# One transpose for queries and keys, one transfer for the row maxima, and a new order of a decoder layer on one core

## What is computed

```
x = layernorm(x + favor_attention(x))         # 16 heads of 16; exp features of 64 per head, kv and its
                                              # sum over each sequence of 128 rows, num/den, then Wo
x = layernorm(x + cross_attention(ctx, x))    # 16 heads of 16, softmax over the 128 rows of ctx
x = layernorm(x + ffn(x))                     # ternary weights 256->1024->256, activations quantized to
                                              # 127 levels by the row's largest magnitude, tanh-based silu
```

## Time and profile before

| | |
|---|---|
| time before, median of 3 runs | 506.53 us (505.39 to 511.43) |
| the profiled execution | 505.92 us, its span 504.2 us |
| mean granted TensorE clock | 0.967 |
| busy: PE / DVE / ACT / POOL | 438.9 / 450.6 / 428.8 / 365.5 us |
| DMA: all packets | 192659, 64.27 MB, mean 127 GB/s |

### The profile page before, as it was taken

How to read it: one execution, slowest core, us unless ns; L and a number is a source line. 1 busy time by engine, 2 the same in 40 slices (tenths; PEclk the granted TensorE clock), 3 DMA queues, 4 the chain that set the end, 5 groups by cost and what they waited for, 6 DMA issues and landing times.

```text
span 504.2 us, 18524 instructions
## 1 busy us (share of the span) xinstructions
PE 438.9 (87%) x6566; PEld 304.7 (60%) x6566; DVE 450.6 (89%) x1355; ACT 428.8 (85%) x908; POOL 365.5 (72%) x789
## 2 busy tenths in 40 slices
PE   4568888998999998999999999999999999876641
PEld 2235666666776766776767676777676766543310
DVE  4667686999999999899999999999999999999771
ACT  2247789999999998999999999999999999867532
POOL 1447767778788888788888888888888876763422
PEclk9979899999999999999999999999999999999875
DMA  7665566787768787566666666666666687542212
GB/s 186 230 125 101 133 116 109 107 154 124 127 130 134 157 140 133 133 146 146 146 146 141 140 139 135 144 140 142 136 145 136 137 139 127 85 75 62 55 33 63
DMA packets 192659, 64.27 MB, mean 127 GB/s; under 512 B 172384, under 2 KB 192352, under 8 KB 192608
## 3 DMA queue, kind: packets, MB, share of 16 engines
q1 hardware_dynamic: 190080, 60.46, 60.4%
q10 hardware_dynamic: 2528, 3.15, 1.7%
HBM read 17.31 MB, written 4.19 MB: 43 GB/s over the span
## 4 chain that ended last, share of the span: by engine, by line
PE 58%; ACT 13%; DMA 11%; DVE 7%; issue 5%; SPq 3%; POOL 3%; ACTq 0%; POOLq 0%; DVEq 0%
PE bank L1131 10%; PE bank L1335 9%; DMA tT<-pkT 4%; PE bank L1306 4%; PE bank L1225 4%; PE bank L1362 4%; PE bank L1183 3%; DMA ffn_ld<-in_L_ffn_w_down_dram 3%; PE bank L1204 2%; PE bank L1145 2%; PE bank L1240 2%; PE bank L1322 2%; PE bank L1150 2%; PE bank L1211 2%; PE bank L1294 2%
## 5 line engine op out<-in xcount | busy, mean ns | idle before, releaser
L1131 PE MATMUL bank<-wq_hi,xT 128*128 128x512 f16 (+1 forms) x256 | 72.5, 338 | 3.7 <-DVE vv L816 2.3
L434 POOL TENSOR_TENSOR ve<-mv,lneps 128x1 f32<-128x1 f32 x96 | 19.4, 202 | 63.4 <-DVE mv L866 48.0
L438 POOL TENSOR_TENSOR rs<-ve,mhalf 128x1 f32<-128x1 f32 x96 | 55.0, 573 | 0.0
L946 DVE SCALAR_TENSOR_TENSOR g<-th,bank 128x512 f32<-128x512 f32 x64 | 43.4, 678 | 4.7 <-ACT th L653 4.3
L558 ACT ACTIVATE x<-y,nmr,rs 128x256 f32<-128x256 f32 x64 | 39.8, 622 | 7.9 <-DVE y L1007 4.4
L630 ACT ACTIVATE pT<-bank 128x512 f32<-128x512 f32 x64 | 37.8, 591 | 9.7 <-PE bank L1296 8.1
L897 DVE TENSOR_REDUCE negm<-bank 128x4 f16<-128x512 f32 x64 | 43.4, 678 | 1.6 <-PE bank L1260 1.2
L898 DVE TENSOR_REDUCE negm<-bank 128x4 f16<-128x512 f32 x64 | 43.5, 680 | 0.0
L577 ACT ACTIVATE phk<-bank 128x512 f32<-128x512 f32 x64 | 39.4, 617 | 4.5 <-PE bank L1150 4.5
L1131 PE MATMUL bank<-wq_lo,xT 128*128 128x256 f16 (+1 forms) x128 | 43.2, 337 | 0.0
L425 POOL TENSOR_TENSOR pkA<-qk,pkA 128x512 f16<-128x512 f32 x32 | 37.6, 1175 | 7.0 <-ACT pkA L520 6.6
(11 more groups left out here) (184 smaller groups left out, 1580.0 us busy)
## 6 DMA issues: line engine op xcount, KB each, us to landing
xs<-in_x_dram SPq DMA_DIRECT2D x32, 128.0 KB, 2.3
cs<-in_ctx_dram SPq DMA_DIRECT2D x32, 128.0 KB, 2.3
xr<-in_x_dram SPq DMA_DIRECT2D x32, 128.0 KB, 2.3
out_dram<-ot SPq DMA_DIRECT2D x32, 128.0 KB, 1.8
ffn_ld<-in_L_ffn_w_gate_dram ACTq DMA_DIRECT2D x1, 1024.0 KB, 9.0
ffn_ld<-in_L_ffn_w_up_dram ACTq DMA_DIRECT2D x1, 1024.0 KB, 11.5
ffn_ld<-in_L_ffn_w_down_dram ACTq DMA_DIRECT2D x1, 1024.0 KB, 13.8
pkAT<-pkA SPq DMA_TRANSPOSE x64, 3.2
```

The source lines that it names most:

```text
L438: g.tensor_tensor(rs[n - 1][:, :], ve[n - 1][:, :], mhalf[:, :], ALU.pow).then_inc(done[f"pw{n}"], 1)
L946: v.scalar_tensor_tensor(g1[:, n, :], th[:, n, :], 1.0, gate, ALU.add, ALU.mult).then_inc(done[f"gl{n}"], 1)
L1131: last = T.matmul(o, xT[:, 2 * part + c, :], w[:, c, cols], start=(n == 0), stop=(n == 5))
```

## The change

- `qT` and `kT` become one DMA transpose of 128 x 2048, `qT`, at the place of the old `qT`; it waits for `lo`, `nlo` and for `phq1` of the tile before. `kT` and its semaphores are gone.
- The row maxima go into 16 packed columns (negm of 128 x 16, not 128 x 128), their transpose has 16 rows (nmT), and `row` is one DMA from these 16 rows into partitions 32 and 96.
- The banks are given out anew, and with them the waits that protect them; some waits and increments that others imply are dropped.
- Every engine's order is new: `LAGS` is 14, `FIRST` is 18. Much of the shift of lags is only where an iteration is said to begin. What moves against its neighbours: on PE `phk0` and `phk1` go behind `s0`, `kvp` goes ahead, `st0` behind `nump`, `vm` to the end; on ACT `p0` goes ahead of `x2_`, `th0` ahead of `x1_`, `sq` behind `x1T_`, `kvm_` before it, `hm1` ahead of `hm0`, `ot_` between `ephq0` and `ephq1`; on POOL `lo` goes ahead of `xqf`, `xb_` two iterations earlier; on SP the order is qT, tT_, load_x, store, cT_, load_r, load_c, hqT_, row. The ffn preparation is spread otherwise over the first iterations.

The core of the diff (the lists of the engines shown for SP and ACT):

```diff
-LAGS = 13
-FIRST = 16
+LAGS = 14
+FIRST = 18
...
-        negm = sb("negm", [P, 2, 64], F16)
+        negm = sb("negm", [P, 2, PAIRS], F16)
...
             def qT(t, par):
-                wait_ahead(sp, t, par, ("phq0", -1))
-                transpose(pkAT[:, 0:PAIRS, :], pkA[:, 0:PAIRS, :, :].rearrange("p c r d -> p (c r d)"), "qT", par)
-
-            def kT(t, par):
-                wait_ahead(sp, t, par, ("lo", 0), ("nlo", 0), ("phk0", -1))
-                transpose(pkAT[:, PAIRS:H, :], pkA[:, PAIRS:H, :, :].rearrange("p c r d -> p (c r d)"), "kT", par)
+                wait_ahead(sp, t, par, ("lo", 0), ("nlo", 0), ("phq1", -1))
+                transpose(pkAT[:, :, :], pkA[:, :, :, :].rearrange("p c r d -> p (c r d)"), "qT", par)
...
             def row(t, par):
                 wait(sp, "mT", t)
-                for p in (32, 96):
-                    sp.dma_start(tT[p:p + 1, par, :, :], nmT[p:p + PAIRS, :]).then_inc(moved["row"][par], 16)
+                sp.dma_start(tT[32:P:64, par, :, :], nmT[:, :]).then_inc(moved["row"][par], 16)
...
-                go(load_c, i, par, 4)
-                go(load_r, i, par, 4)
+                go(qT, i, par, 4)
+                go(tT_, i, par, 7)
                 go(load_x, i, par, 0)
-                go(kT, i, par, 3)
+                go(store, i, par, 14)
+                go(cT_, i, par, 6)
+                go(load_r, i, par, 2)
+                go(load_c, i, par, 5)
                 go(hqT_, i, par, 10)
-                go(store, i, par, 13)
                 go(row, i, par, 7)
-                go(qT, i, par, 3)
-                go(tT_, i, par, 6)
-                go(cT_, i, par, 5)
```

More of the change, by code:

```diff
@@ L561, in x1_ @@
             def x1_(t, par):
+                wait(act, "rs1", t)
                 wait(act, "ya2", t, -2)
@@ L672, in iteration @@
             def iteration(i, par):
[L673 to L683, removed]
                 go(aT, i, par, 4)
-                go(kvm_, i, par, 3)
+                go(thi, i, par, 5)
                 go(xT_, i, par, 0)
-                go(thi, i, par, 5)
-                go(ot_, i, par, 11)
                 once(evacuate[1], i, 5)
@@ L691, in iteration @@
                 go(nT_, i, par, 3)
+                go(p0, i, par, 6)
                 go(x2_, i, par, 7)
-                go(p0, i, par, 6)
                 go(vh, i, par, 5)
-                go(ephk1, i, par, 2)
[L696 to L700, removed]
+                once(evacuate[2], i, 5)
+                go(hi, i, par, 1)
+                go(hm1, i, par, 8)
+                go(oxT_, i, par, 6)
+                go(ephk0, i, par, 2)
+                go(ephk1, i, par, 2)
+                once(evacuate[3], i, 5)
                 go(hm0, i, par, 8)
-                go(hm1, i, par, 8)
                 go(xqT_, i, par, 7)
+                go(ephq0, i, par, 2)
+                go(ot_, i, par, 10)
+                go(ephq1, i, par, 2)
+                go(th0, i, par, 7)
+                go(x1_, i, par, 4)
+                once(evacuate[4], i, 6)
+                go(mT, i, par, 5)
+                go(th1, i, par, 7)
+                once(evacuate[5], i, 6)
+                go(x1T_, i, par, 4)
+                once(evacuate[0], i, 3)
+                go(kvm_, i, par, 2)
+                go(sq, i, par, 0)
             run(act, iteration)
@@ L1360, in dn @@
                 wait_moved(pe, "hqT", t, par)
+                wait(pe, "v", t, 8)
                 for k in range(8):
@@ L1407, in iteration @@
-                once(ternaries[1], i, 5)
-                go(dn, i, par, 9)
-                once(ffn_means, i, 2)
-                go(st1, i, par, 6)
-                go(st0, i, par, 6)
-                go(nump, i, par, 3)
-                go(wo, i, par, 4)
-                go(vhp, i, par, 5)
+                go(mTp, i, par, 6)
+                go(u0, i, par, 8)
+                if isinstance(i, int) and i == 7:
+                    pe.wait_ge(done["ephq0"], 5)
+                once(ternaries[5], i, 7)
@@ new lines, in iteration @@
+                go(kvp, i, par, 3)
+                go(x1Tp, i, par, 5)
+                go(xTp, i, par, 0)
+                go(aTp, i, par, 4)
+                go(u1, i, par, 8)
+                once(ffn_means, i, 2)
+                go(tm, i, par, 5)
+                go(dn, i, par, 9)
+                go(st1, i, par, 6)
+                go(nump, i, par, 3)
+                go(st0, i, par, 6)
+                if isinstance(i, int) and i == 5:
+                    pe.wait_ge(done["ephq0"], 3)
+                once(ternaries[1], i, 5)
@@ new lines, in iteration @@
+                go(wo, i, par, 4)
+                once(ternaries[0], i, 3)
+                if isinstance(i, int) and i == 5:
+                    pe.wait_ge(done["ephk1"], 3)
+                once(ternaries[2], i, 5)
+                go(vhp, i, par, 5)
+                if isinstance(i, int) and i == 5:
+                    pe.wait_ge(done["v"], 5)
+                once(ternaries[3], i, 5)
+                go(ntp, i, par, 3)
+                go(pv1, i, par, 6)
+                go(pv0, i, par, 6)
@@ new lines, in iteration @@
+                go(s0, i, par, 5)
+                go(phk0, i, par, 2)
+                go(phk1, i, par, 2)
+                go(qkm, i, par, 0)
+                go(oxp, i, par, 6)
+                go(phq0, i, par, 2)
+                go(xqTp, i, par, 7)
+                go(phq1, i, par, 2)
+                go(s1, i, par, 5)
+                go(kvs, i, par, 2)
+                go(g0, i, par, 7)
+                if isinstance(i, int) and i == 6:
+                    pe.wait_ge(done["qk"], 7)
+                once(ternaries[4], i, 6)
```

249 lines of the change are left out of this document (101 added, 148 removed), and 8 rows, old and new, of the table done.

## The result

The changed kernel took 515.67 us (median of 4 runs, 514.67 to 516.55), the kernel before beside it 506.62 (505.39 to 511.43). The ratio is 1.0147, 95% interval 1.0087 to 1.0208: slower by 1.5%, clear of no change.

What follows compares the result with a forecast made beforehand. PE, DVE and ACT were taken as full at once, no period below DVE's 12.98 us, the tT loop becoming the bound by a hair at 13.12. 505.9 + 3.0 (full part) - 2 (filling) - 3 (draining) = 503.9, said as 504; range 495 to 518.

Steps and rivals of the forecast that it cites:

- the sentence on GpSimd's order: On POOL, `lo` delays `xqf` by 1.2 us, at the edge: costed at nothing, up to 0.2 us a period if passed.
- Rival 3: Order costs elsewhere, by an edge wait such as `xqf` behind `lo`: 0.2 us over 26 periods, 509 us; chance 0.16.
- DVE's work: DVE's busy time from tile 9 to 31, taken as a floor under any order's period: 12.98 us.
- The wide transpose: On SP, the 128 x 2048 transpose: issue about 2.4 us, 1.13 more than the half; landing at 4.5 us.
- the fewer engines for 16 rows: New `row` DMA might use 2 engines against 8 for each old one, reaching `st1` a little later; not in the sum.
- Rival 1: Wide transpose's data start only after its issue, landing after 5.8 us: 13.7 us a period, about 518.5 us; chance 0.14.
- The tT loop: Loop from `s0` through `st1`, `p1`, `mT`, `row`, qT and tT to the next but one `s0`: 26.24 us per two periods.
- The unrolled part: Unrolled iterations before the hardware loop: plus 0.9 us for a late landing, 0.7 for `FIRST` of 18.
- a late landing not cushioned: One late tT landing in unrolled periods, where the loop lacks 0.24 us instead of having 0.69 to spare: 0.9 us.
- The filling: Start of the kernel, while the pipeline fills: minus 2 us, between minus 6 and plus 2.
- The gate: In the filling, PE's matmul of the three sums (28.67), before `phk` of tile 0: nothing gained there.
- The draining: End of the kernel, `p0` ahead of `x2_` and `th0` ahead of `x1_` on ACT: minus 3 us, between minus 1 and minus 5.

Runs made afterwards that it cites:

- e7: Changed kernel with `lo` made of two instructions of 128x256 (queries, keys) instead of one of 128x512, nothing moved: ratio 1.0053 to the kernel before.
- e5: Changed kernel with `qnt` (the step xm) moved behind `m0` on DVE, GpSimd's order untouched: ratio 1.0206 to the kernel before.
- e1: Changed kernel with `lo` behind `xqf` again on GpSimd, as in the kernel before: ratio 1.0009 to the kernel before.
- e3: Kernel before with one line moved, `lo` ahead of `xqf` on GpSimd: ratio 1.0134 to the kernel before.
- e6: Changed kernel with `lo` behind `xqf` on GpSimd and `qk_` behind `rx` and `sg` on DVE: ratio 1.0017 to the kernel before.
- e9: e6 with `FIRST` 14 instead of 18, four periods moved from unrolled code into the hardware loop: ratio 0.9977 to the kernel before.
- e8: e6 with two transposes of 128x1024, keys first, at the place of the one of 128x2048: ratio 1.0212 to the kernel before.
- e10: e6 with `FIRST` 22 instead of 18, four more periods unrolled: ratio 1.0074 to the kernel before.
- e12: e6 with ACT's two pairs as before, `x2_` ahead of `p0` and `x1_` ahead of `th0`: ratio 1.0201 to the kernel before.

## Why the prediction was wrong

The forecast was 504 us, faster by 0.5%; it came out 1.5% slower. Point by point:

- **The step that failed** is the sentence on GpSimd's order: "On POOL `lo` now delays `xqf` by its 1.2 us [...] costed at nothing, and at up to 0.2 us a period if the edge is passed." I asked only who waits for `xqf`, not what runs beside `lo`. It put `lo` beside xm, and xm's 0.90 us more go into the one engine that I had called full at 12.98 (e7, e5, e1). What the runs showed in place of "at nothing" is some 0.47 us a period by this wait inside xm (13.55 against 13.08 in e7, where half of the wait is gone). And even the wait that I did ask for was nearly twice my bound, 0.35 us a period in the kernel before (e3). Rival 3 had the place right (`xqf` behind `lo`), at 0.2 us and 509 us; it had neither the mechanism nor the size.
- **DVE's busy time is no fixed floor.** "No order can take a period below DVE's work, which is 285.5 / 22 = 12.98 us" read too much into busy time. With the same 41 DVE instructions a period the new order without the collision is busy from tile 19 to 31 for 152.8 us, 12.73 a period (e6; 12.71 in e1):

```profile
242.60:399.30 156.70, 154.78 (x2426) 111.19 (x2436) 152.77 (x493) 153.87 (x337) 134.11 (x288) 1.00 0.68 141
```

  So the new order had freed some 0.25 us of DVE a period, and the collision took that and more. That is why the period rose by 0.54 and not by the whole 0.90.
- **The trace of before had shown it**, and I passed over it. While the pipeline fills, DVE and GpSimd in order of time:

```profile
48.47 1.35 POOL L438 TENSOR_TENSOR rs<-ve,mhalf 128x1 f32<-128x1 f32 x1
...
48.56 1.23 DVE L794 TENSOR_SCALAR ffn_ld<-ffn_t 128x2048 f32<-128x2048 f32 x1
```

  The small `rs` takes 0.55 us at the median. Closer still, `nlo` took 0.93 us at 40.88, beside `lo`, where its median is 0.30. A DVE or GpSimd instruction with two durations for one shape can hold a wait that no column shows. What this looks like is a page's rule: the Trainium skill, page SBUF — State Buffer, section Who interferes with whom, says that VectorE and GpSimd share one pair of SBUF ports, that a VectorE `tensor_scalar` from SBUF to SBUF may take it, and that whoever issues first holds it for the whole instruction while the other stands still. For xm and `lo` the runs agree (1.25 us behind a whole `lo`, 0.76 behind half of one, 0.34 and GpSimd delayed where xm came first). For `rs` they do not: in the rows above `rs` started 0.09 us first by the records and yet it was the one that waited, and in every loop period before xm ran inside `rs` and neither was slowed:

```profile
257.80 0.56 POOL L438 TENSOR_TENSOR rs<-ve,mhalf 128x1 f32<-128x1 f32 x1
...
257.93 0.34 DVE L942 TENSOR_SCALAR xm<-x,arec 128x256 f32<-128x256 f32 x1
```

  So the rule says where to look in the two lists before anything runs, and that the price can be as much as the other instruction's duration; whether a pair collides the trace has to say.
- **The wide transpose** was costed at 2.4 us of SP and 4.5 to landing; in the loop it took 1.8 to 2.05 and 4.3 to 4.5; in the unrolled part of the changed kernel the landing was 5.0 at the median and up to 6.3. `row` took 0.56, not 0.7, and no wait for it is left among PE's from tile 9 on (3.8 us in ten periods before), so the fewer engines for 16 rows that I had named cost nothing that shows. Rival 1 (data only after the issue, 5.8 us) was wrong, since the data moved 0.9 us before the issue was over; that the time came near its 518.5 is chance.
- **The tT loop** was forecast at 13.12 a period, with PE waiting for tT before `s0` in most of them. With the collision out of the way the period is 13.04 to 13.06 (e6, e9), and e8 shows that some 0.6 us more on SP lengthen it, so the loop exists and lies close. That it sets the period is not shown: between 272 and 394 us of e6 no matmul waits for tT and the weight loads only 0.9 us in all, and SP stood 3.3 us, in eight of nine periods, until DVE's `tlo` let it issue tT. The nearness of 13.12 is partly luck, and what holds e6 at 13.05 was not isolated. (Two roundings in the recorded sums, 0.24 for 0.22 us here and 518.5 for 518.8 us in rival 1, change nothing.)
- **The unrolled part** was forecast at 0.9 (a late landing not cushioned) and 0.7 (`FIRST`). It is plus 4.7, of which e6, without the collision, still has 4.0. The waits for tT there are what I had described, but many: 7 of ten periods, 6.6 us of matmul time, against 4 and 2.7 before. tT's own landing is 4.1 to 4.2 us there (3.7 before). A term of the right kind, 2.5 times too small.
- **The filling** was forecast at minus 2 and is plus 3.1. The gate stood where I said (`ffn_means` at 28.60, 28.67 before). After it, between 39 and 44 us, DVE's `nhi` and `nlo` collided with GpSimd's `lo` and `phe`: 1.21 and 1.16 us where their medians are 0.32 and 0.30. Both lie on the chain that ended last. But `nhi` and `nlo` took 0.19 and 0.93 in this place before, so they make some 1.2 of the 3.1 us at most. That is read from the trace and no run isolates it; and since e6, e9 and e10, equal up to there, differ by 1.2 us at tile 9, cause and size of this part stay open.
- **The draining** was forecast at minus 3 and is minus 3.7; e12 takes it back, so mechanism and size were right. What the forecast lacked is that ACT's new order is worth 0.34 us a period in the full part too (e12 against e6).

So one gain is shown by runs, ACT's order, some 4 us in the draining (and as much in the full part). One is read from the trace alone, the shorter `row`. The wide transpose beats two narrow ones at its place, and no run compares it with the old arrangement. Against this the collision takes 6.2 us of span by e7, and the mostly unrolled stretch from tile 9 to 19 takes 4. The best version here has `lo` behind `xqf`, `qk_` late and `FIRST` 14: ratio 0.9977, interval 0.9943 to 1.0012, which is not yet told from the kernel before.

## What to carry to other kernels

Before a step is moved on GpSimd or VectorE, look at what will run beside it on the other, not only at who waits for it, and look in the trace for instructions with two durations for one shape: such a wait counts as busy time and has no releaser. A busy time is then not the engine's work either, and no floor under the period. If a full engine has got "busier" with the same work, compare its groups by line, minimum against median. Where such a collision is found, move one of the two behind or ahead of the other, or cut the longer one in two, and ask at once what stands next: here each cure brought a wait of 0.3 to 0.6 us of its own, and one of them lost in the draining what it won in the full part.

## What the hardware showed that I had not expected

- Behind a GpSimd instruction, xm ended 0.15 us after that one's end (0.14 by the rounded rows above), both for `lo` (1.16 us) and for its half (0.67). So 0.2 of its 0.34 us ran while it stood there, or before; which, the records do not say. In e7 xm's recorded start is even 0.03 us ahead of the half's, and it still waited; where it was 0.05 us or more ahead it did not.
- In the kernel before xm ran beside GpSimd's `rs` of 128x1 (257.80 to 258.36) and took 0.34 us, as in nearly every other tile: not every overlap in the records is a collision.
- The issue of a DMA transpose does not grow in step with its width: 1.25 us for 1024 columns, 1.8 to 2.05 for 2048 in the looped part.
- Unrolled code cost 0.7 us a period more than the same steps in the hardware loop (e6, e9, e10), and 0.37 in the kernel before.
